# A new order of work in the first narrow attention layer: transposes in one run, queries and keys at the end of a step and three batches ahead

## The reference, cut to what matters

```python
q = (x @ Wq + bq).reshape(B, Tx, HEADS, HEAD_DIM).transpose(0, 2, 1, 3)
k = (xf @ Wk + bk).reshape(B, Txf, HEADS, HEAD_DIM).transpose(0, 2, 1, 3)
v = (xf @ Wv + bv).reshape(B, Txf, HEADS, HEAD_DIM).transpose(0, 2, 1, 3)
scores = jnp.einsum('bhqd,bhkd->bhqk', q * SCALE, k)
probs = jax.nn.softmax(scores, axis=-1)
attn = jnp.einsum('bhqk,bhkd->bhqd', probs, v)
out = attn.transpose(0, 2, 1, 3).reshape(B, Tx, D)
out = out @ Wo + bo
```

## Time and profile before

| what | value |
|---|---|
| median of three runs | 1865.37 us (1864.48 to 1868.91) |
| profiled execution, its own time | 1865.58 us |
| its span in the trace | 1863.8 us |
| PE busy | 1801.1 us, 97% |
| DVE, ACT, POOL busy | 1367.3, 1238.3, 678.7 us |
| the changed stage | 958.2 to 1179.2 us |

### The profile page before, as it was taken

The page is one execution under the profiler, slowest core; times in us unless marked ns, Lnnn a source line. Parts: engine busy times, 40 slices in busy tenths (PEclk is TensorE's granted clock), DMA queues, the critical chain, the costliest instruction groups (busy, mean ns, idle before and its releaser), DMA issues. The chain is left out here.

```text
span 1863.8 us, 53731 instructions
## 1 busy us (share of the span) xinstructions
PE 1801.1 (97%) x19100; PEld 1552.4 (83%) x19100; DVE 1367.3 (73%) x2604; ACT 1238.3 (66%) x3855; POOL 678.7 (36%) x943
## 2 busy tenths in 40 slices
PE   8999999999999999998989999999999999999997
PEld 7889888887988889887977777787888888888885
DVE  5767767665776767666758888657888888888886
ACT  5666666664666666664348888536777778777776
POOL 3433333334434434433322222454343434343431
PEclk9999999999999999999999999999999999999999
DMA  8100000000000000000000000000000000000000
GB/s 230 24 0 0 0 0 0 0 2 1 2 0 0 0 0 0 0 1 2 0 1 1 0 0 0 2 1 1 4 6 3 4 3 4 3 4 3 5 4 8
DMA packets 18437, 14.88 MB, mean 8 GB/s; under 512 B 4466, under 2 KB 16308, under 8 KB 18356
## 3 DMA queue, kind: packets, MB, share of 16 engines
q1 hardware_dynamic: 18356, 13.78, 2.8%
HBM read 11.68 MB, written 2.10 MB: 7 GB/s over the span
## 5 line engine op out<-in xcount | busy, mean ns | idle before, releaser
L967 POOL TENSOR_TENSOR L0a_probs<-L0a_probs,L0a_inv_sum 128x1024 f32<-128x1024 f32 x64 | 121.4, 1897 | 212.8 <-DVE L0a_inv_sum L819 212.8
L967 POOL TENSOR_TENSOR L0b_probs<-L0b_probs,L0b_inv_sum 128x1024 f32<-128x1024 f32 x64 | 121.4, 1896 | 125.2 <-DVE L0b_inv_sum L819 125.2
L1690 ACT ACTIVATE L2L_w_probs<-L2L_scores,L2L_w_neg_max 128x128 f32<-128x128 f32 x256 | 92.0, 395 | 77.1 <-DVE L2L_w_neg_max L1848 77.1
L2058 POOL TENSOR_TENSOR L2L_w_probs<-L2L_w_probs,L2L_w_inv_sum 128x1024 f32<-128x1024 f32 x64 | 121.3, 1896 | 33.6 <-DVE L2L_w_inv_sum L1884 33.6
L677 ACT ACTIVATE L0a_qT<-L0a_ring 128x512 f32<-128x512 f32 x64 | 38.3, 598 | 126.9 <-PE L0a_ring L533 126.9
L677 ACT ACTIVATE L0b_qT<-L0b_ring 128x512 f32<-128x512 f32 x64 | 38.3, 598 | 125.7 <-PE L0b_ring L533 125.7
L830 DVE COPY L0b_v<-L0b_ring 128x512 f32<-128x512 f32 x64 | 44.3, 692 | 94.0 <-PE L0b_ring L563 94.0
L830 DVE COPY L0a_v<-L0a_ring 128x512 f32<-128x512 f32 x64 | 44.3, 692 | 93.2 <-PE L0a_ring L563 93.2
L2027 POOL TENSOR_TENSOR L2L_w_x_bias<-x,bias_L 128x128 f32<-128x128 f32 x32 | 14.6, 456 | 239.9 <-DVE x L1928 239.9
L1701 ACT ACTIVATE L2L_n_probs<-L2L_scores,L2L_n_neg_max 128x128 f32<-128x128 f32 x256 | 90.9, 420 | 7.0 <-DVE L2L_n_neg_max L1854 6.9
L1233 DVE TENSOR_REDUCE L_row_max<-L_scores 128x8 f32<-128x1024 f32 x64 | 78.1, 1220 | 23.0 <-PE L_scores L1095 23.0
(11 more groups left out here) (260 smaller groups left out, 5804.9 us busy)
## 6 DMA issues: line engine op xcount, KB each, us to landing
out_x<-x SPq DMA_DIRECT2D x32, 64.0 KB, 1.5
x<-in_x SPq DMA_DIRECT2D x1, 512.0 KB, 4.2
L0a_wq<-in_L_xattn_Wq SPq DMA_DIRECT2D x1, 512.0 KB, 5.4
L0a_wk<-in_L_xattn_Wk SPq DMA_DIRECT2D x1, 512.0 KB, 6.2
L0a_wv<-in_L_xattn_Wv SPq DMA_DIRECT2D x1, 512.0 KB, 6.7
L0a_wo<-in_L_xattn_Wo SPq DMA_DIRECT2D x1, 512.0 KB, 7.7
L0b_wq<-in_L_xattn_Wq SPq DMA_DIRECT2D x1, 512.0 KB, 4.9
L0b_wo<-in_L_xattn_Wo SPq DMA_DIRECT2D x1, 512.0 KB, 7.0
```

Source lines behind the costliest of these rows:

```text
L967: nc.gpsimd.tensor_tensor(to, to, inv_sum[:, :, s, :].unsqueeze(3) .to_broadcast([TOKENS, 2, GROUP, TOKENS]), ALU.mult).then_inc(divided, 1)
L1690: done = nc.scalar.activation(w_slot(at, 0)[:, h, :], scores[:, 0, r, i, :], ACT.Exp, scale=W.scale, bias=w_neg_max[:, h:h + 1], accum_out ...
L2058: nc.gpsimd.tensor_tensor(to, to, w_inv_sum[:, :, s, :].unsqueeze(3) .to_broadcast([TOKENS, 2, GROUP, TOKENS]), ALU.mult).then_inc(w_divid ...
```

## The change

The order of the operations within a step is changed on all engines, and some are done for a later batch:

- PE: all four groups of transposes stand together behind the scores, and the output projection behind them. Queries and keys move to the end of the step, and are those of batch `t + 3` (before: `t + 2`). The rows that are turned are those of `t + 4` (before: `t + 3`). In step -1 ten matmuls on the identity are added ahead of the first scores.
- ACT: queries and keys are copied out behind the exponentials.
- DVE: the second row maxima stand ahead of `finish`.
- POOL: rows first, four ahead, then context and keys, three ahead.
- The pipeline starts a step earlier (-4), and the loop covers steps 3 to 26 instead of 3 to 28.

```diff
--- before.py
+++ after.py
@@ -1002,10 +1002,10 @@
 
 
 
-    order = [("T0", 0, "act"), ("T1", 0, "act"), ("Wo", -1, "dve"), ("T2", 0, "act"), ("T3", 0, "act"),
-             ("qk", 2, "act"), ("v", 1, "dve"), ("hT", 3, "dve"), ("sum", 0, "dve"), ("PV", 0, "dve")]
-    first, last = -3, BATCHES
-    steady_first, steady_last = 3, BATCHES - 4
+    order = [("T0", 0, "act"), ("T1", 0, "act"), ("T2", 0, "act"), ("T3", 0, "act"), ("Wo", -1, "dve"),
+             ("v", 1, "dve"), ("hT", 4, "dve"), ("sum", 0, "dve"), ("PV", 0, "dve"), ("qk", 3, "act")]
+    first, last = -4, BATCHES
+    steady_first, steady_last = 3, BATCHES - 5
     ring = Ring(order, range(first, last + 1), BATCHES, {})
     GROUP = 4
     QUAD = DIM // 4
@@ -1149,25 +1149,24 @@
                                            start=True, stop=True), "Wo")
 
             def step(t):
+                if t.n == -1:
+                    keep_clock(nc, scores[:, 0, 0, 0, :], ident, START_COUNT)
                 if here(t, 1):
                     score(t.plus(1))
                 if here(t, 0):
-                    transpose_probs(t, 0)
-                    transpose_probs(t, 1)
+                    for n in range(4):
+                        transpose_probs(t, n)
                 if here(t, -1):
                     project_out(t.plus(-1))
-                if here(t, 0):
-                    transpose_probs(t, 2)
-                    transpose_probs(t, 3)
-                if here(t, 2):
-                    queries_keys(t.plus(2))
                 if here(t, 1):
                     values(t.plus(1))
-                if here(t, 3):
-                    transpose_h(t.plus(3))
+                if here(t, 4):
+                    transpose_h(t.plus(4))
                 if here(t, 0):
                     weigh("sum", t)
                     weigh("PV", t)
+                if here(t, 3):
+                    queries_keys(t.plus(3))
 
             steps(pe, step)
 
@@ -1209,12 +1208,12 @@
                 if here(t, 0):
                     for n in range(4):
                         turned_probs(t, n)
-                if here(t, 2):
-                    projections(t.plus(2))
                 if here(t, 1):
                     exponentiate_0(t.plus(1), 0)
                     exponentiate_0(t.plus(1), 1)
                     exponentiate_1(t.plus(1))
+                if here(t, 3):
+                    projections(t.plus(3))
 
             steps(act, step)
 
@@ -1273,14 +1272,14 @@
                 if here(t, 1):
                     row_maxima(t.plus(1), 0)
                     negate_maxima(t.plus(1))
+                    row_maxima(t.plus(1), 1)
                 if here(t, -1):
                     finish(t.plus(-1))
                 if here(t, 1):
-                    row_maxima(t.plus(1), 1)
                     subtract_maxima(t.plus(1))
                     values(t.plus(1))
-                if here(t, 3):
-                    turned_h(t.plus(3))
+                if here(t, 4):
+                    turned_h(t.plus(4))
                 if here(t, 0):
                     divide(t)
 
@@ -1311,14 +1310,11 @@
                                         ALU.mult).then_inc(keys_apart, 1)
 
             def step(t):
+                if here(t, 4):
+                    copy_rows(t.plus(4))
                 if here(t, 3):
-                    copy_rows(t.plus(3))
-                if here(t, 3) and not here(t, 1):
                     stage_context(t.plus(3))
-                if here(t, 2):
-                    set_keys_apart(t.plus(2))
-                if here(t, 3) and here(t, 1):
-                    stage_context(t.plus(3))
+                    set_keys_apart(t.plus(3))
 
             steps(pool, step)
```

## The result

The changed kernel took 1872.32 us (median of 10 runs, 1867.43 to 1875.22), the kernel before 1866.67 us on the same chip (10 runs, 1864.48 to 1868.91). The ratio is 1.0027, with a 95% interval of 1.0018 to 1.0037: about 5 us slower, just under the 0.3% from which the prediction speaks of slower. It had forecast 1871.4 us in a range of 1866 to 1875.

A forecast was written before the change was run, and what follows sets the result against it. ACT's loop was taken to bound each step before the change (6.49 us) and PE's chain after it (6.64 us). Steady part +2.5 and start +3.5 made +6.0 us: 1871.4 us against the median, range 1866 to 1875.

The forecast's parts named there:

- What bounds the step: Steady step: ACT's loop falls from 6.49 to 6.07 us, and PE's chain of 6.64 us becomes the bound.
- The forecast's signs: Steps 6.55 to 6.7 us; no ACT wait before scores; 0.2 and 0.17 us idle around queries and keys; sums' wait 0.5 or more.
- The tail: PE behind the weighted values: 0.20 us switch plus 0.66 for queries, keys and the switch to scores, 0.86 us together.
- The start of the sums: PE in each steady step: row sums still start at +4.07 us, tied to ACT's fourth copy, which doesn't move.
- The turn of the loop: Steady steps: those outside the loop, without register computation, were put 0.07 us lower, 6.57 instead of 6.64 us.
- The steady part: The 29 middle steps: 24 at 6.64, 4 at 6.57, one at 6.07, 191.7 against 189.2 us, +2.5 us.
- The start: Stage start: later queries and keys and ten warming matmuls delay the first scores; +1.7 to +5.6 us, taken as +3.5.
- The cheap start: Rival at the stage start: warming matmuls and transposes run mostly at full clock, +1.7 us, 1869.6 us; chance 0.22.
- The late bank: Rival at each step's end: DVE frees the values' bank over 0.27 us later, PE waits; 1877 us; chance 0.07.
- The end: From the last scores on: no queries or keys in either kernel, tied to ACT's copies; costs nothing.
- The sum: Whole kernel: +2.5 steady and +3.5 start make +6.0 us, 1871.4 us against the median.
- 28 steps at 6.43 and one at 6.07: Gain rival's threshold: PE's tail under 0.65 us instead of 0.86 saves the start's 3.5 us; gain's chance 0.11.

The follow-up runs named there:

- e2: Changed kernel plus one unused identity matmul (two passes) between queries and keys at the end of each step; ratio 1.0041 to the kernel before.
- e3: Changed kernel plus the same unused matmul between row sums and weighted values, bringing two more tile-width changes; ratio 1.0085 to the kernel before.
- e11: Kernel before with all four transpose groups together, output projection behind them and DVE's finish behind the second row maxima; ratio 0.9988 to the kernel before.
- e8: Changed kernel run once more, unaltered, to see how much a trace varies; ratio 1.0018 to the kernel before.
- e1: Changed kernel without the ten warming matmuls ahead of the first scores; ratio 1.0000 to the kernel before.
- e6: Changed kernel with values between transpose pairs, queries and keys before the row transpose, their ACT copies between exponentials, no warming; ratio 0.9944 to the kernel before.

## Why the prediction was right or wrong

**What bounds the step: right.** ACT's 0.42 us left its loop, and PE's chain took its place as the bound. The forecast's signs are in the rows: no wait for ACT ahead of the scores, 0.20 us idle ahead of queries and keys and 0.17 (at the turn) or 0.13 behind them. e2 and e3 show it by what they add. The expected wait of 0.5 us or more ahead of the sums came out at 0.41.

**The tail: right in size.** From the end of the weighted values to the next scores 0.86 us were forecast (0.20 + 0.66). Measured: 0.89 at the turn (1049.10 to 1049.99) and 0.85 in the other step (1055.76 to 1056.61; e2 has 1054.10 to 1055.18, 1.08, with 0.23 for its pair, so 0.85 too).

**The start of the sums: mis-sized.** The step of the prediction that failed is "the sums still start at +4.07": it took from the trace of before a length, the four copies', that the change itself shortened by joining the transposes. They start at +3.95, and the steps of the loop without the turn take 6.51 instead of 6.64. e11 shows the shortening of the copies without the rest of the change. I had treated the move of `project_out` as free of effect.

**The turn of the loop: not foreseen.** 11 turns cost 0.15 us each in the changed kernel, +1.7 us, where the kernel before pays 0.07 x 12 = 0.8. The prediction put 0.07 us for the loop on each of its steps; by row maxima a step without the turn takes 6.51 in the loop and 6.50 outside it.

The steady part added up, by row maxima: 12 steps at 6.51 where 6.64 stood (-1.6), 11 at 6.66 (+0.2), four at 6.50, one at 6.41 and the last at 5.98 where 6.64, three times 6.57, 6.57 and 6.07 stood (-0.6). Together -1.9: +0.6 us instead of the forecast's +2.5.

**The start: mis-sized, within its bounds.** Forecast +3.5 (1.7 to 5.6), measured +4.7 and, in e8, +4.3. The chain on PE up to the first scores was as worked out: the second pair of queries and keys begins 6.27 us behind the opening in e1, where 964.45 - 958.23 = 6.22 was forecast, and the first scores stand at +10.67 and, in e8, at +11.69, where 967.3 to 969.9 is +9.07 to +11.67. The middle value was too kind: the warming ran at 1.2 GHz for most or all of its length in these two. The cheap start, +1.7, came in no trace with ten: e2, whose ten ran at 2.4 GHz, has +3.9 (with its pairs of passes).

**The late bank: it didn't cost anything to speak of, but the 0.27 us of margin were gone.** DVE freed the bank of the values 0.13 us before PE took it (1049.17, 1049.30). The reckoning left out that a load follows such a release by 0.115 us, as in e11, and the sums' earlier start took the other 0.12. Weighted values that ended earlier still would have met this wait. **The end** cost nothing, as forecast (-0.1 us).

**The sum.** +6.0 was forecast; the stage shows +5.1 (e8: +4.7), the ratios say +5.0 and +3.4. It came out this near by luck in part: the steady part was put 1.9 us too high and the start 1.2 too low. (Among the rivals, 28 steps at 6.43 and one at 6.07 save 3.1 us and not the 3.5 said there; nothing else rests on it.) That the total was close says less for the working than the rows of the tail do.

## What to carry to other kernels

When work is moved off the engine that binds, look at where it lands on the others: here ACT's 0.42 us were worth 10.5 us in all where PE's four passes stood ahead of a wait that PE had anyhow (e6, which also moves the values), and nothing where they stood behind the last thing that it does (e1), both without warming. Lengths of groups in an old trace hold only as long as their feeders are not touched; a chain that joins or splits them has to be worked out again, piece by piece. A warming put ahead of a chain that nothing hides costs its own length, here 2.3 and 3.5 us, against 1.0 and 2.5 that it gave back. And a wait that the trace puts down to one engine is best held against the waits in the program: in e11 the release that counted was another engine's.

## What was not expected of the hardware

The number of matmuls ahead of a loop changed the cost of its turn on PE. Ten of them, in place of none or seven, made the step behind the branch 0.09 to 0.12 us longer in the changed kernel (6.57 and 6.54 to 6.66), and 0.15 longer in the kernel before (6.56 to 6.71); e11, e2 and e3 had no surcharge at all. No DMA packet goes with it, and its cause is open. Over the loop that is 1 to 2.3 us, as much as many a change is worth, and a comparison of two orders carries it as a hidden term. Four copies by ACT ended 2.18 us behind their start when the transposes came in two groups and 2.06 to 2.07 when they came in one; the next instruction's start moved less (2.07 to 2.05).
